# Stacked attentions: the value and denominator matmuls of two units are issued together in every second slot

## The reference

```python
x = x + xattn(layernorm(x), ctx, ...)        # ctx: 64 x 120 x 128, 16 heads of 8
# one attention:
scores = einsum('bhqd,bhkd->bhqk', Q, K) / sqrt(8)   # plus a mask in some layers
attn = softmax(scores, axis=-1)
out = einsum('bhqk,bhkd->bhqd', attn, V)
return out.reshape(B, L, 128) @ Wo + bo
```

## Time and profile before

| | us |
|---|---|
| median of 3 runs | 4264.2 |
| lowest and highest run | 4257.89, 4265.51 |
| the profiled execution's time | 4260.05 |
| its span (first to last instruction) | 4258.2 |
| PE busy in the span | 3539.6 |
| DVE busy | 3346.6 |
| ACT busy | 2332.4 |
| POOL busy | 1570.1 |

### The profile page before, as it was taken

One profiled execution on the slowest core, in us unless ns is written; L12 is line 12 of the kernel. 1 busy time (PEld: TensorE's weight loads), 2 busy tenths in 40 slices (PEclk: granted clock), 3 DMA queues, 4 the chain that ended last, 5 costly groups with the idle time before them and its releaser, 6 DMA issues. The chain is left out here.

```text
span 4258.2 us, 95393 instructions
## 1 busy us (share of the span) xinstructions
PE 3539.6 (83%) x31830; PEld 2463.6 (58%) x31831; DVE 3346.6 (79%) x6141; ACT 2332.4 (55%) x4244; POOL 1570.1 (37%) x911
## 2 busy tenths in 40 slices
PE   6983979999599899993058849999499998799999
PEld 3552646667476566662046626666365666677777
DVE  7888879998898788885035578888687877788888
ACT  2432657775376566651035536777566665466665
POOL 2210045553000454533744435554254443222222
PEclk9985989998699899995579969999699999799999
DMA  1002122222000222220112142221221112100000
GB/s 63 16 31 103 76 61 64 62 65 63 13 0 6 63 60 57 60 69 13 52 56 62 57 123 62 58 60 49 69 50 47 46 47 73 40 13 12 15 15 15
DMA packets 158984, 209.04 MB, mean 49 GB/s; under 512 B 37820, under 2 KB 109824, under 8 KB 155585
## 3 DMA queue, kind: packets, MB, share of 16 engines
q1 hardware_dynamic: 150593, 189.40, 16.4%
q0 software_dynamic: 8192, 16.92, 1.2%
HBM read 53.09 MB, written 42.21 MB: 22 GB/s over the span
## 5 line engine op out<-in xcount | busy, mean ns | idle before, releaser
L704 ACT ACTIVATE a_p<-a_p 128x480 f32<-128x480 f32 x832 | 501.8, 603 | 517.7 <-DVE a_p L552 515.2
L348 POOL TENSOR_TENSOR a_km<-a_k,a_slots 96x1920 fp32r<-96x1920 f32 x186 | 631.9, 3416 | 176.9 <-DMA a_k<-a_kh 176.9
L547 DVE TENSOR_REDUCE a_mx<-a_sc 128x4 f32<-128x480 f32 (+1 forms) x832 | 542.6, 652 | 124.4 <-PE a_sc L792 95.1
L552 DVE TENSOR_TENSOR a_p<-a_sc,a_mx 128x480 f32<-128x480 f32 x832 | 531.4, 639 | 18.8
L710 ACT ACTIVATE a_pt<-a_tp 120x512 f32<-120x512 f32 x832 | 487.7, 586 | 81.6 <-PE a_tp L801 76.6
L801 PE MATMUL a_tp<-ident,a_p 128*120 128x128 f32 x3328 | 509.7, 276 | 4.1 <-ACT a_p L704 2.3
L801 PEld LDWEIGHTS a_tp<-ident,a_p 128*120 128x120 f32 x3328 | 399.6, 138 | 90.0 <-ACT a_p L704 27.5
L786 PE MATMUL a_sc<-a_km,a_qr 96*128 96x480 f32 x768 | 395.1, 514 | 32.3 <-DMA a_qr<-a_ql 29.4
L825 PE MATMUL a_nd<-a_pt,a_vm 120*32 120x128 f32 x6656 | 354.6, 285 | 0.0
L825 PE MATMUL a_nd<-a_pt,a_dm 120*32 120x128 f32 x6656 | 334.4, 273 | 0.0
L1767 ACT ACTIVATE f_s<-f_pu 128x512 f32<-128x512 f32 x256 | 153.4, 599 | 212.6 <-PE f_pv L1249 212.6
(11 more groups left out here) (429 smaller groups left out, 8911.6 us busy)
## 6 DMA issues: line engine op xcount, KB each, us to landing
a_qr<-a_qh SPq DMA_DIRECT2D x384, 64.0 KB, 2.0
a_k<-a_kh SPq DMA_DIRECT2D x384, 60.0 KB, 2.0
a_ctx<-in_ctxT SPq DMA_DIRECT2D x64, 240.0 KB, 2.7
a_qr<-a_ql SPq DMA_DIRECT2D x192, 64.0 KB, 2.0
a_k<-a_kl SPq DMA_DIRECT2D x192, 60.0 KB, 2.0
dispatched<-f_empty SPq DMA_DIRECT2D x8, 1040.0 KB, 21.1
f_xr<-dispatched SPq DMA_DIRECT2D x32, 260.0 KB, 2.6
chosen<-f_none SPq DMA_DIRECT2D x8, 1024.0 KB, 11.9
```

Of the source, the lines that this page charges most:

```text
L348: v.tensor_tensor(KM[par][:, i, :, :].rearrange("p b (j k) -> p b j k", k=KN), K3[:, i, :, :].unsqueeze(2).to_broadcast([TR, GB, 4, KN]), ...
L547: v.tensor_reduce(mx[:], view, AX.X, ALU.max).then_inc(mx_ready, 1)
L552: v.tensor_tensor(PR[s % 4][:].rearrange("p (h k) -> p h k", k=k), view, mx[:].unsqueeze(2).to_broadcast([P, heads, k]), ALU.subtract).the ...
L704: a.activation(PR[s % 4][:], PR[s % 4][:], ACT.Exp).then_inc(exp_ready, 1)
```

## The change

In the stacked attentions (`U` = 4) `values` is no longer called in every slot. Even slots have none. In odd slots it is called for the units s - 5 and s - 4 together, first the value matmuls of the one and the other, then the denominator matmuls of the one and the other. `values` gets an argument that says which of the two kinds it does, and only the denominator call tells `pv_done`. Each call has its own wait for `pt_ready`. a0 (`U` = 1) keeps its order. No matmul is added or removed, and no other engine's order is touched.

```diff
-                def values(g, s, par):
+                def values(g, s, par, whats=(0, 1)):
...
-                    for what in range(2):
+                    for what in whats:
...
-                    last.then_inc(pv_done, 1)
+                    if 1 in whats:
+                        last.then_inc(pv_done, 1)
...
-                    if not (first and s < VALUES) and s - VALUES < S:
-                        values(g, s - VALUES, par if s >= VALUES else 1 - par)
+                    if U == 1:
+                        if not (first and s < VALUES) and s - VALUES < S:
+                            values(g, s - VALUES, par if s >= VALUES else 1 - par)
+                    elif s % 2 == 1 and not (first and s < VALUES) and s - VALUES < S:
+                        two = (s - VALUES - 1, s - VALUES)
+                        for what in range(2):
+                            for u in two:
+                                values(g, u, par if s >= VALUES else 1 - par, (what,))
```

## The result

The changed kernel takes 4199.22 us (median of 4 runs, 4196.66 to 4201.81), the kernel before 4264.85 in the same comparison (4257.89 to 4268.69). The ratio is 0.9845, with a 95% interval of 0.9833 to 0.9857: 66 us faster. The profiled execution took 4198.75, its span is 4196.9.

The account below looks back on a forecast made before the run. PE was taken to set the pace in a2 and a3, in a1 only by 0.1 us. Braked savings (a1 +5, a2 -24, a3 -30, s3 -18) gave -67, taken as -60: 4204 us, likeliest case 4174 to 4234, 8 in 10 4156 to 4248.

Parts of the forecast that it names:

- The saving on PE per pair: Stacked attentions: one two-unit strip block replaces two blocks, 1.24 us instead of 1.55, saving 0.31 us per pair of slots.
- the bound of 0 of this term: PE's saving is 0 if the 0.20 gap belongs to the operation behind it, not the strip/full-array change.
- The whole of 159: Four stacked attentions: 512 pairs at 0.31 us each save 159 us if all of it reaches the end.
- Brake (1): DVE's total: a1 can gain at most 0.10 us per unit, 25 us; a2, a3 and s3 fit the full 0.155.
- Brake (2): Odd slots' transposes come too early and wait for ACT's exponential, some 0.35 us in a3's slots 2 and 3.
- the walk: Start times worked through 16 slots in both orders: a3 falls from 30.1 to 28.3 us per group.
- The margin of 7 us: Whole kernel: -67 summed, -60 taken, since each engine handover read 0.05 longer takes 13 us off.
- The stall at the end of s3's trips: PE idles at s3's loop ends for an instruction fetch, 6.4 us a trip, six times; forecast to stay.
- The chance of 0.12: Rival: s3's stall goes too because the code shifts, 38 us more, 4166; chance 0.12.
- The whole saving (4119): Rival: brakes hold nothing; a2, a3 and s3 save all and a1 25, together 145 us, 4119; chance 0.05.
- Slower by bursts: Rival: DVE runs out of scores while PE is in 16 strips, 4297 to 4331; chance 0.07.
- the 38 named: Rival: loops of a1, a2, a3 catch s3's stall, 38 us each; chance 0.02 for one, 0.02 for two or more.

Follow-up runs that it names:

- experiment 1: Changed kernel with the odd slot's transposes between the two units' strip blocks, so as many strip/full-array changes as before: 4231.04 us, ratio 0.9922.
- experiment 4: Kernel before, plus 160 already fulfilled waits (80 instructions) ahead of PE's loop in s3: 4231.87 us, ratio 0.9922.
- experiment 2: Changed kernel plus 64 already fulfilled waits (32 instructions) ahead of PE's loop in s3: 4166.09 us, ratio 0.9769.
- experiment 8: Changed kernel with a1 left unpaired as before, only a2, a3 and s3 paired: 4189.92 us, ratio 0.9829.
- experiment 9: Changed kernel with strips unit by unit, a1 unpaired, 160 waits ahead of s3's loop: 4160.25 us; beside it, a2, a3, s3 projections in odd slots: 4209.27 us.
- experiment 5: Experiment 1's kernel plus 64 fulfilled waits ahead of PE's loop in s3: 4234.55 us, ratio 0.9932; its table lists loop places and stalls.
- experiment 3: Changed kernel plus 180 already fulfilled waits (90 instructions) ahead of PE's loop in a3: 4191.13 us, ratio 0.9835.

## Why the prediction was right

**The saving on PE per pair.** Right: 0.31 forecast. From the first scores of a pair of slots to those of the next, as the median over the loop's groups, the pairs of a3 in which nobody waits went 4.09 to 3.76, 4.07 to 3.75, 3.58 to 3.26 and 4.17 to 3.85, 0.32 or 0.33 each. One part was off: I took 0.03 for whatever follows transposes, but an output or a projection stands 0.109 behind them. The output's own two records then start 0.12 apart instead of the 0.22 they have behind strips (2705.28 and 0.39 here, 2702.16 and 0.49 in the earlier trace rows), so that the sum came out the same. That the gap belongs to the change and not to the operation, the bound of 0 of this term, is what experiments 1 and 4 show: the same number of changes, no gain (ratio 0.9922 both), and 0.203 between strips and transposes. Whether it is the strips' width, their place in the array or the way they share it that costs the 0.20, no run tells apart. The sentence of the Trainium skill that I drew on, that a change of tiling mode drains TensorE, stands in "TensorEngine Tiling (Array Packing)" under Key Properties, not in the Overview; it agrees with a gap at every change in either direction, and the 0.40 per pair worked out beside it was 0.32.

**The whole of 159, less two brakes.** The order of the brakes was right in each phase: +5, -24, -30 and -18 forecast, +3.0, -23.8, -31.0 and -14.0 measured; with the stall taken away on both sides s3 gives -17 (experiments 2 and 4). Brake (1): a1, where DVE had 0.10 per unit left, got nothing, and experiment 8 gave back 2.3 us. That DVE's fullness is the reason is read from the waits; no run changes DVE's work in a1. Brake (2): slots 2 and 3 of a3 went from 3.51 to 3.58, the walk had 3.52 to 3.65. The walk of a group of a3 after the change, 3.79, 3.65, 3.39, 4.04, 2.97, 3.40, 3.86, 3.22, was measured as 3.76, 3.58, 3.39, 3.75, 3.26, 3.42, 3.85, 3.17: one pair 0.3 too long and the next 0.3 too short, as in its walk of before, and 28.3 against 28.2 in all. That the sum is right to 0.1 is thus in part luck. (The two sums of the walk differ by 1.82 us, 0.114 per unit or 29 us for a3, not the 0.117 and 30 that I wrote.) The wait for the exponential that it foresaw is there twice a group. That ACT's copy of the keys causes it holds only in part: with the copy a slot later slots 2 and 3 gained 0.13 and the pair behind lost 0.19.

In s3 the sum hides a brake that I had not seen. With the stall away on both sides (experiment 4, then 2) slots 0 and 1 went up from 3.91 to 4.49, some 9 us in 16 groups, while five of the other pairs gained 0.23 to 0.34. The four pieces of the layer norm in slot 0, in experiment 4 and then in experiment 2:

```profile
3225.14 1.02 DVE L151 TENSOR_SCALAR s_h<-x,s_mean,s_rstd 128x128 f32 x4
```

```profile
3228.55 1.60 DVE L151 TENSOR_SCALAR s_h<-x,s_mean,s_rstd 128x128 f32 x4
```

In the faster order POOL is still at the masked keys when DVE comes to them: one piece lasts 0.80 us or more in 14 groups of experiment 2 and in none of experiments 4 and 1, and PE then waits for them at slot 1 (9.7 us, 12 times). It is the meeting of experiment 9, and the change made it.

**The margin of 7 us** between -67 and the -60 I took was about right in size (the span fell by 61.3), though it does not stand where I put it: the attentions gave 65.8, and the 4 us elsewhere are within what executions differ by, so that the fit is partly luck too.

**The stall at the end of s3's trips.** Forecast to stay at 6.4 us a trip, six times; it stayed (3.65 idle), and to be without it is worth 6.0 a trip and 35.8 in s3 of the kernel before (experiment 4) and 6.6 and 38.6 in the changed one (experiment 2), where the rival had 38. The chance of 0.12 was a guess about a place that I couldn't see, and the table of experiment 5 shows how near it was: unit by unit, the same change comes without the stall and at 4167.

**The rivals.** The whole saving (4119) fell with the brakes. "Slower by bursts" did not happen with two units, though DVE's idle time, forecast to carry it, did fall from 51.6 to 31.6 in a3; with four units it happened, 4369, beyond the 4331 that I had given for the worst of it. No loop of a1, a2 or a3 caught a stall by the change; experiment 3 shows that it could have, at 29.7 us instead of the 38 named, since a3 has less slow work behind the idle stretch: its slots 0 and 1 take 1.6 us more there than elsewhere, those of s3 2.5 (before) and 3.0 (changed).

## What to carry to other kernels

Count the changes between strips and the full array in PE's order, not only its matmuls: each pair of changes that goes is worth a fixed time, 0.32 us here, where PE sets the pace, and was worth nothing in a1, where DVE had hardly any slack. A faster order also moves where the other engines meet: look for instructions that grew longer. How long PE may be away is bounded by the work that its consumer holds in its buffers; two units were inside it, four were not. When a kernel with loops gets faster or slower by a few tens of us, look at the ends of its trips before crediting the edit, since the place of the code alone made as much here as half of the change.

## What the hardware showed that I had not expected

- A strip matmul behind full-array work, or the reverse, starts 0.201 to 0.205 us later in nearly all of several hundred cases and never sooner, and full-array work behind transposes 0.028 (scores) or 0.109 (projection, output).
- Sixty-four fulfilled waits in PE's code, 32 instructions, moved the time by 33 us; a loop of 6.3 times 256 instructions stalls 3.7 us at each trip's end or not at all by its place, with 9 transfers of 16 KB a trip when it does (61 in 6.9 trips) and one to four in 350 or 360 us when it doesn't. The same place can stall in one kernel and not in another, or in half of the trips.
- DVE's `TENSOR_SCALAR` of 128x128, of which three more follow in 0.77 us, lasted until 0.08 or 0.09 after the end of the POOL instruction that it met, 128 times of 128: 2.56 and 0.82 us in the two shown, where 0.34 is usual. With the projections of s3 in other slots this, and the lower clock behind PE's idle time, cost 49 us.
